# Attention stage with three banks for the row-maximum scores and one for the probability products

## The reference, cut to what matters

```python
kv_lat = xn @ W_kvd
q_lat = xn @ W_qd
...
kk = jnp.concatenate([k, k_rope], axis=-1)
qq = jnp.concatenate([q, q_rope], axis=-1)
scores = jnp.einsum('bqhd,bkhd->bhqk', qq, kk) * scale
scores = jnp.where(causal[None, None], scores, jnp.finfo(scores.dtype).min)
probs = jax.nn.softmax(scores, axis=-1)
y = jnp.einsum('bhqk,bkhd->bqhd', probs, v).reshape(B, S, H)
return y @ W_o
```

## Time and profile before

| | |
|---|---|
| runs | 4331.84, 4334.64, 4338.19 us, median 4334.64 |
| profiled execution | 4341.7 us, its span 4339.9 us |
| mean granted clock of TensorE | 0.939 |
| attention stage | to about 1,715 us of the span |
| busy over the whole span | PE 3742.1, VectorE 2956.6, ScalarE 2513.7, GpSimd 2196.6 us |

### The profile page before, as it was taken

The page is one execution under the profiler, slowest core; times in us unless marked ns, Lnnn a source line. Parts: engine busy times, 40 slices in busy tenths (PEclk is TensorE's granted clock), DMA queues, the critical chain, the costliest instruction groups (busy, mean ns, idle before and its releaser), DMA issues. The chain is left out here.

```text
span 4339.9 us, 70850 instructions
## 1 busy us (share of the span) xinstructions
PE 3742.1 (86%) x22264; PEld 2767.9 (64%) x22264; DVE 2956.6 (68%) x5456; ACT 2513.7 (58%) x6505; POOL 2196.6 (51%) x1115
## 2 busy tenths in 40 slices
PE   5888888888888874899969999998999998999986
PEld 2344444444444442777758888887888887888876
DVE  3454454555444522222259999999999999999998
ACT  1443343434343441233358888888888888888874
POOL 3223333333333322000038788778778778878774
PEclk8899998999898987999989999999999999999998
DMA  3322222222232312666622212212222222222221
GB/s 91 98 80 84 80 92 86 88 80 81 79 101 81 93 46 75 199 208 208 211 92 98 88 68 100 93 66 97 93 70 93 93 81 82 93 88 75 93 83 38
DMA packets 286365, 417.03 MB, mean 96 GB/s; under 512 B 78261, under 2 KB 250678, under 8 KB 263672
## 3 DMA queue, kind: packets, MB, share of 16 engines
q1 hardware_dynamic: 273048, 381.12, 27.2%
q0 software_dynamic: 12288, 33.57, 2.2%
q10 hardware_dynamic: 864, 0.10, 0.0%
HBM read 330.63 MB, written 83.17 MB: 95 GB/s over the span
## 5 line engine op out<-in xcount | busy, mean ns | idle before, releaser
L1536 POOL TENSOR_TENSOR m_ub<-m_Bb,m_dtx 128x2048 f32<-128x2048 f32 x254 | 1156.9, 4566 | 280.3 <-PE m_Y L1904 176.4
L1645 ACT ACTIVATE m_dA<-m_dt,m_a_neg 128x128 f32<-128x128 f32 x4096 | 1211.1, 388 | 129.4 <-DVE m_S L1756 129.0
L1904 PE MATMUL m_Y<-m_ub,m_ident 128*128 128x128 f32 x8192 | 955.8, 278 | 62.4 <-DVE m_ub L1733 62.0
L1904 PEld LDWEIGHTS m_Y<-m_ub,m_ident 128*128 128x128 f32 x8192 | 939.3, 194 | 73.1 <-DVE m_ub L1733 72.8
L543 ACT ACTIVATE f_pt<-f_X 128x512 f32<-128x512 f32 (+1 forms) x704 | 371.8, 555 | 730.3 <-PE f_X L845 699.1
L618 DVE TENSOR_REDUCE f_nm<-f_Y 128x1 f32<-128x512 f32 (+3 forms) x896 | 434.0, 531 | 378.3 <-PE f_Y L845 354.1
L1748 DVE SCALAR_TENSOR_TENSOR m_PR<-m_dA,m_S 128x512 f32<-128x512 f32 x512 | 355.9, 695 | 25.7 <-POOL m_ub L1536 7.4
L1748 DVE SCALAR_TENSOR_TENSOR m_S<-m_dA,m_PR 128x512 f32<-128x512 f32 x512 | 354.8, 693 | 12.0
L1756 DVE CUSTOM_DVE_ANT_1 m_S<-m_S,m_ub 128x512 f32<-128x512 f32 x512 | 353.3, 690 | 0.6 <-issue 0.6
L1756 DVE CUSTOM_DVE_ANT_1 m_PR<-m_PR,m_ub 128x512 f32<-128x512 f32 x512 | 353.3, 690 | 0.2 <-DVE m_PR L1748 0.2
L828 PE MATMUL f_Y<-f_kst,f_qst 96*128 96x512 bf16 (+3 forms) x1024 | 256.2, 331 | 109.0 <-DVE f_nm L618 90.4
(11 more groups left out here) (234 smaller groups left out, 6369.2 us busy)
## 6 DMA issues: line engine op xcount, KB each, us to landing
m_Bb<-m_bc_dram SPq DMA_DIRECT2D x64, 1024.0 KB, 4.6
m_Cb<-m_bc_dram SPq DMA_DIRECT2D x64, 1024.0 KB, 6.4
f_parts_dram<-f_parts SPq DMA_DIRECT2D x32, 768.0 KB, 4.1
f_kst<-f_parts_dram SPq DMA_DIRECT2D x192, 128.0 KB, 2.6
f_qst<-f_parts_dram SPq DMA_DIRECT2D x192, 128.0 KB, 2.6
e_rows<-sorted_rows SPq DMA_DIRECT2D x70, 256.0 KB, 2.8
e_wg<-Wg SPq DMA_DIRECT2D x70, 256.0 KB, 2.9
e_wu<-Wu SPq DMA_DIRECT2D x70, 256.0 KB, 4.0
```

Of the source, the lines that this page charges most:

```text
L1536: pool.tensor_tensor(ub[:, h, i, :, :], Bb[:, s, :, :], dtx[:, m, None, s * SN:(s + 1) * SN].to_broadcast([P, NST, SN]), ALU.mult).then_in ...
L1645: last = act.activation(dA[:, h, i, n, :], dtt[:, par, m, s * SN:(s + 1) * SN], ACT.Exp, scale=a_neg[:, m, n:n + 1])
L1904: last = pe.matmul(Y[:, i * SN:(i + 1) * SN], ident[:, :], ub[:, h, 1 + i, n, :], start=False, stop=(n == NST - 1), skip_group_check=True)
```

## The change

Ring Y gets three banks, the products get one in place of two; eight banks in all as before. `place` numbers the fills of a ring anew in each round (bank = number % depth), and counts the uses of each bank over the rounds, so that the semaphores' values hold with three banks. `oc` of a group no longer stands behind the first `pv` of the second block of keys of the next group, but behind the third `s2` of that group's first block: four skeleton entries earlier, ahead of the next group's first `pv`. That `pv` now waits for this copy. `first_pair` is counted from the `oc` of group 1, and goes from 39 to 35: the six items of pair 0 move four entries earlier. Since the skeleton entry `oc` stands earlier, the items of `AT` between its old and its new place stand one `s2` earlier than before.

```diff
-    BANKS = {ring: [pb(f"f_{ring}{i}", [P, SEQ]) for i in range(2)] for ring in ("X", "Y", "Z")}
-    O = [pb(f"f_O{i}", [P, SEQ]) for i in range(2)]
+    DEPTH = {"X": 2, "Y": 2, "Z": 2, "Y": 3}
+    BANKS = {ring: [pb(f"f_{ring}{i}", [P, SEQ]) for i in range(DEPTH[ring])] for ring in ("X", "Y", "Z")}
+    O = pb("f_O", [P, SEQ])
...
             if n == min(2, N_S2[kb]) - 1 and q > 0:
                 S2_ITEMS.append(("pv", q - 1, 0))
-                if kb == 1 and g > 0:
-                    S2_ITEMS.append(("oc", g - 1, 0))
+            if n == 2 and kb == 0 and g > 0:
+                S2_ITEMS.append(("oc", g - 1, 0))
...
+        depth = DEPTH[ring]
+
+        def uses(m, bank):
+            return (len(NUMBERS[m, ring]) + depth - 1 - bank) // depth
         n = index(r)
         if isinstance(n, int):
-            n = sum(len(NUMBERS[m, ring]) for m in range(FIRST, n)) + NUMBERS[n, ring][k]
-            return n % 2, n // 2
-        first = sum(len(NUMBERS[m, ring]) for m in range(FIRST, FULL))
-        n = first + (r[1] - FULL) * len(NUMBERS[FULL, ring]) + NUMBERS[FULL, ring][k]
-        return n % 2, r[0] * len(NUMBERS[FULL, ring]) + n // 2
+            at = NUMBERS[n, ring][k]
+            bank = at % depth
+            return bank, sum(uses(m, bank) for m in range(FIRST, n)) + at // depth
+        at = NUMBERS[FULL, ring][k]
+        bank = at % depth
+        first = sum(uses(m, bank) for m in range(FIRST, FULL)) + (r[1] - FULL) * uses(FULL, bank) + at // depth
+        return bank, r[0] * (2 * uses(FULL, bank)) + first
...
-                act.activation(yT_[:, parity(kind, r), i, :], O[i % 2][:, :], ACT.Copy).then_inc(o_copied, 1)
+                act.activation(yT_[:, parity(kind, r), i, :], O[:, :], ACT.Copy).then_inc(o_copied, 1)
...
             if kb == 0:
-                if g >= 2 or not isinstance(b, int) or b > 0:
-                    pe.wait_ge(o_copied, NG * b + g - 1)
+                if g > 0 or not isinstance(b, int) or b > 0:
+                    pe.wait_ge(o_copied, NG * b + g)
```

More of the change, by code:

```diff
@@ L225, in build_attn @@
     const_ready = sem("f_const_ready")
-    ring_full = {ring: [sem(f"f_{ring}_full{i}") for i in range(2)] for ring in BANKS}
-    ring_free = {ring: [sem(f"f_{ring}_free{i}") for i in range(2)] for ring in BANKS}
+    ring_full = {ring: [sem(f"f_{ring}_full{i}") for i in range(DEPTH[ring])] for ring in BANKS}
+    ring_free = {ring: [sem(f"f_{ring}_free{i}") for i in range(DEPTH[ring])] for ring in BANKS}
     x_loaded = sem("f_x_loaded")
@@ L852, in values @@
             if kb == 0:
-                if g >= 2 or not isinstance(b, int) or b > 0:
-                    pe.wait_ge(o_copied, NG * b + g - 1)
+                if g > 0 or not isinstance(b, int) or b > 0:
+                    pe.wait_ge(o_copied, NG * b + g)
             src = pt[:, PT_W:] if q % 2 else pt[:, 0:PT_W]
             for j in range(HG):
-                last = pe.matmul(O[g % 2][j * VA:(j + 1) * VA, kb * P:SEQ], va[:, kb, g * HG + j, :], src[:, j * n:(j + 1) * n],
+                last = pe.matmul(O[j * VA:(j + 1) * VA, kb * P:SEQ], va[:, kb, g * HG + j, :], src[:, j * n:(j + 1) * n],
                                  start=(kb == 0), stop=(kb == TT - 1), tile_position=(0, j * VA))
```

## The result

The changed kernel takes 4373.56 us (median of 5 runs, 4369.65 to 4380.0) against 4338.19 us of the kernel before (5 runs): 1.0079 of it, 95% interval 1.0062 to 1.0097. It is slower by 35 us where 25.7 us less were forecast. The profiled execution takes 4380.0 us.

The account below looks back on a forecast made before the run. PE was taken to bound the kernel, with only its idle time to win. Terms of 9.3, 4.4, 10.9, 1.1 and 0 us summed to 25.7 us less, 4308.9 us against the median of 4334.64; range 4284 to 4337.

Parts of the forecast that it names:

- The views: Reading of the profile before: PE makes up a round, only its idle time can be won, Y waits mostly hide others.
- Pair 0's items earlier: Odd rounds: pair 0's shares load earlier, so VectorE waits less for pair 1's sums; 9.3 us won, bounds 0 and 16.5.
- The drain: Round 14: pair 1's sums go from store to load sooner, so PE waits less for `yT`; 4.4 us won, bounds 0 to 8.3.
- The third bank: Two Y waits between `ht` and `nmt` go in 14 rounds, less a router wait; 10.9 us won, bounds 0 to 14.8.
- absorbed: Rival: PE only reaches the next chain sooner and waits there; 4329 to 4334.6 us, chance 0.14.
- the price of a wait: Y waits ahead of `T` or `ht` counted 0, as PE would wait for `h1` or `h2` anyway.
- The cast of `nm`: Pair 0's reciprocal leaves the place ahead of VectorE's first `nm` cast; 0 net, bounds -4 and +27 us.
- The escape: The `nm` cast starts ahead of GpSimd's subtraction and escapes its delay, 27 us more; rival of more gain, chance 0.10.
- The clock as a rival: Merged PE waits ahead of `ht` lower TensorE's clock behind them, up to 6.1 us a round; slower, chance 0.08.
- the case priced at 14 us slower: Clock rival with half of the 13 rounds newly at the lower clock behind `ht`: 14 us slower, 4349 us.

Follow-up runs that it names:

- e1: The changed kernel with ring Y back at two banks, keeping the changed order and the single product bank: 4362.41 us, 1.0047 of the kernel before.
- e3: The changed kernel plus useless matmuls in PE's waits each round (12 ahead of `T`, 12 before `ht`, 8 ahead of `nmt`): 4298.71 us.

## Why the prediction was wrong

*The views.* "Nothing here makes a matmul shorter" is where it begins to go wrong: the change makes them longer. The reading of waits was right: of the 129 Y waits most went, and those for `h1` and `h2` took their place.

*Pair 0's items earlier, 9.3 us.* The mechanism was right. In round 9 after the change:

```profile
1000.44 0.58 SPq L410 DMA_DIRECT2D f_shares<-f_shares_dram  x1
...
1023.08 0.57 SPq L400 DMA_DIRECT2D f_sums_dram<-f_yT  x1
...
1025.04 0.34 SPq L403 DMA_DIRECT2D f_sums<-f_sums_dram  x1
```

1.96 us from store to load, 8.46 before; VectorE's wait for the sums is down from 18.2 us in 8 to 6.3 in 1. It isn't on the path any more, though: in the changed kernel 28.4 us lie between the `nmt` of round 8 and the `T` of round 9 as before, of which 3.1 went to the low clock behind `nmt` (6.6 for 3.5 us). e1, with two Y banks, shows the gain: 25.9 us in odd rounds from 5 on, 26.6 to 28.4 before. Its even rounds gave it back at the loop's turn.

*The drain, 4.4 us.* `wo` of round 14 waits 5.29 us in place of 8.30: 3.0 where 4.4 were said. Round 14 gave more than was summed, 76.9 us in place of 87.5: a wait of 4.63 us for ScalarE ahead of its last `pv`, which no term had, is gone as well, Y waits fell by 1.2 us, and the clock is 0.93 where it was 0.90.

*The third bank, 10.9 us.* The waits at the two places are gone, but PE arrives at the next chain sooner by as much and waits there; that is the rival "absorbed", which I priced at no loss. The step that failed is the price of a wait: I set a Y wait of 1 to 2 us ahead of `T` or `ht` at nothing since another would take its place. In one piece it costs the clock behind it as well: 3.1 us behind `nmt`, some 6 us behind `ht` in 9 of the 12 rounds of the loop. Nor does the prediction have a term for PE's wait for ScalarE ahead of `ht` (`f_X`, 1.43 us in round 8 before, 3.63 after).

*The cast of `nm`.* 0, as said. It starts still right behind GpSimd's subtraction and takes 2.10 us. The escape didn't happen. The wait ahead of `nmt` I had at 0 net; it grew by 0.5 us and brought a low clock with it.

*The clock as a rival.* It was named, with its right mark (clock under 0.94: 0.87), and a chance of 0.08. Its price, up to 6.1 us a round behind `ht`, was near: there the low clock lasts over 10 us in 3 of rounds 2 to 13 before and in 9 after, half of them more, which is the case priced at 14 us slower. That 14 is 39.7 us lost less the 25.7 forecast; the loss came about (35 us in all), the gain didn't. That the two numbers are so near is in part luck, since `nmt` and `T` have a share in the low time that the rival left out, and 1.3 us a round is idle time. What I held against the rival, that both levels are seen behind a 0.86 us wait, is true, and true of the wait ahead of it too. In rounds 8 and 10 of the kernel before:

```profile
945.19 0.39 PE L834 MATMUL f_X<-f_qst,f_kst 99*128 99x512 bf16 x1 [1.43 <-ACT f_pt L543]
946.86 1.09 PE L778 MATMUL f_Z<-f_ident,f_h 128*128 128x128 f32 x8 [0.86 <-ACT f_h L566]
...
1145.71 0.39 PE L834 MATMUL f_X<-f_qst,f_kst 99*128 99x512 bf16 x1 [1.42 <-ACT f_pt L543]
1147.38 1.96 PE L778 MATMUL f_Z<-f_ident,f_h 128*128 128x128 f32 x8 [0.86 <-ACT f_h L566]
```

The same waits, and the full clock behind them once and the lower level once. It doesn't follow that long waits are free: with 3.6 us in place of 1.4 the clock is low behind `ht` in all twelve rounds. (The Trainium skill's "TensorE: Matmul & The Clock Gate", section "A second HAM failure mode: psum-queue depth-cycling", which warns of short idle times between groups, bears here: the clock does go down and up several times a round. That fewer such stops would help isn't borne out: PE's Y waits fell from 90.4 to 28.1 us, and the clock from 500 to 700 us from 0.94 to 0.87.) Against the loss stood 25.7 / 14 = 1.8 us a round that I had to give.

*Not foreseen.* The stop at the loop's turn goes away when 40 tiny matmuls stand at PE's start, and that gave 10 to 15 us.

## What to carry to other kernels

Here a deeper ring didn't take waits away; it handed them to the next chain, in larger pieces. Before adding a bank, list what PE will stand at next and start those chains earlier; here the change lost 29 us by itself, and was 64 us ahead of the two-bank kernel once `bn` came two entries sooner in both. Where PE is the bound, price a wait by the clock behind it too: look at the granted clock in the microseconds after each long wait, and, as a probe, fill the wait with matmuls of no use. If the kernel gets faster, the wait is worth removing at its source, which is often a piece of work on a slower engine that nobody needs yet.

## What the runs showed of the hardware

- In all of rounds 2 to 13 of the changed kernel the granted clock is low behind the single waits of PE of 2.6 to 4.0 us (`nmt`, `ht`, `T`), for some 3 to 13 us. With the wait ahead of `T` filled to 1.2 us it is 1.00 up to `ht` in all of them (e3). The kernel before has one such place too, behind a Y wait of 2.71 us in round 9. Behind waits of 1 to 1.5 us both levels are seen.
- Twelve matmuls of 512 columns that do nothing, in one wait of each round, made a kernel 99 us faster (2.3%); some 15 of these are the stop at the loop's turn, which went with them. The same twelve where PE has no wait made it 15 us slower.
- A loop's turn on PE costs a stop of 2.7 to 3.2 us, or none with the same loop where 40 matmuls more stand ahead of it. What brings it stays open.
